# One transformer layer with a two-of-eight expert feed-forward: expert weight pieces placed singly in the last pass, raw rows kept in the next expert's slot, ranks and scatters moved forward

## The chip, the cores and the metric

The kernel runs on one core of one Trainium2 chip. Its time is the device time of one execution in microseconds (us); the number compared is the median over runs. The core has five engines with a queue each, which run their own instructions in order: TensorE (PE, with its weight loads shown as PEld), VectorE (DVE), ScalarE (ACT), GpSimd (POOL) and SyncE (SP, which here only issues transfers). They meet through semaphores alone.

## The reference, cut to what matters

There are 16 batches of 100 rows of width 512, and for each batch a context of 722 rows of width 384.

```python
x = x + self_attention(layernorm(x))            # 16 heads of 32, rotary, causal
x = x + cross_attention(layernorm(x), ctx_768)  # 16 heads of 32, keys and values from ctx
n = layernorm(x)
gates = softmax(n @ gate_w.T + gate_b)          # 8 experts
top_gates, top_idx = top_k(gates, 2)
expert_out = einsum('bsh,eoh->bseo', n, expert_w) + expert_b
x = x + (take(expert_out, top_idx) * top_gates).sum(experts)
```

## The kernel before, in words

**Passes.** The program is a software pipeline of passes n = -1 to 16. Pass n does the cross attention of batch n and prepares batch n+1 (self attention, keys and values of the context). Each pass is a list of 20 steps (`STEPS`, and for the last two `LAST_STEPS` and `END_STEPS`), and a step is a list of names. Every engine walks the same lists and runs its own part of each name, so the order in the lists is the order in each engine's queue, written out by hand. Pass 15 (`LAST_STEPS`) has no next batch to prepare. Pass 16 (`END_STEPS`) runs the feed-forward for the sorted rows.

**Cross attention of a pass.** It goes by four groups of four heads. For group g: `Ag` and `Bg` are the scores of the two halves of the context on PE (L1009); `max_Ag` and `max_Bg` are row maxima on DVE (L1268), which hold the score banks until they are read; `MXg` turns the joined maximum on PE (L911), ACT copies it (L1084) and DVE splits it (L1224); `Tga` and `Tgb` are the scores turned, each followed by `expga` or `expgb` on ACT (L1111). `highga`/`highgb` (ACT, L1120) and `lowga`/`lowgb` (POOL, L1442) split the probabilities into two half-precision parts, and `PVg` multiplies them with the values (PE, L921). `A` of the next group waits for both `exp` of this one. `PV3` of a pass, `scale_heads` (POOL, L1436), `TT` (turn the heads' output) and `TP` (its projection and the residual) stand in the next pass.

**Chunks.** The other PE work goes through four PSUM banks in turn (`filler`): PE writes a bank, ACT copies the high part, DVE forms the low part and counts `chunk_out`; a chunk's PE work waits until DVE is done with the chunk four before it.

**Experts' weights.** An expert's 512x512 float32 weights are loaded raw (`load_expert`), and four pieces `FWek` turn them on PE (four transposes each, L957), then ACT (L1093) and DVE (L1236) write their two half-precision parts into `wT_all`, the expert's slot in `bank`. Slot e takes the place of weights of the attention that are no longer wanted: slots 0 to 3 of the self attention's four matrices, 4 to 6 of the cross attention's, 6 and 7 of the keys of even passes. Experts 0, 1 and 2 lie raw in their own slot, so ACT waits for all four turned pieces before it writes the first; experts 3 to 7 lie raw in three other places that come free one after another. The pieces stand four at a time in `LAST_STEPS`.

**Routing.** Rows come in 13 tiles: 11 early ones (batches 0 to 13) and two late ones (batches 14 and 15). For tile t: `FSt` statistics (DVE), `FNt` normalising (POOL, L712 to L717), `FXt` turning (PE), `FLt` gate scores. When the eleventh tile is done, `RT00` to `RT03` and `RE0` take the softmax and the two best experts (DVE, L578 to L605; ACT), `RP` writes the picks, `FR` counts them on PE (L970, L973) and `dve_place` on DVE works out each row's place among 29 slot tiles sorted by expert (L627 to L646; L639 writes the places and counts `placed`). `SCt` on POOL (L690) then scatters tile t's normalised rows to DRAM, two indirect transfers a tile; SP brings the rows back into one of four buffers ahead of it (`load_again`), where tile t+4 waits until tile t is scattered. In pass 16 SP loads the sorted slots once all scatters have landed (`end_loads`, L468), and for each slot tile j `STj` (turn, L966) and `SMj` (product, L323) follow. After them come the two late tiles through all experts, and the sums.

## Time and profile before

| | us |
|---|---|
| median of 3 runs (lowest, highest) | 1288.94 (1286.7, 1290.46) |
| profiled execution, its own time | 1286.48 |
| its span, first to last instruction | 1284.7 |
| PE busy over the span | 1196.7 (93%) |
| DVE busy | 835.0 (65%) |
| POOL busy | 728.5 (57%) |
| ACT busy | 641.6 (50%) |

The profile is one execution. Busy shares are means over stages with different limits, so each stage has to be read by itself: passes -1 to 14 up to 1036 us, pass 15 from there to about 1120 us, pass 16 and the sums to the end. In the chain of waits each step stands at the instruction that ended last or at what released it, and "issue" is time in which an engine waited for nothing that the profile shows.

### The profile page before, as it was taken

To read this page: it belongs to the slowest core of one execution; us is meant where nothing else is said; L and a number is where in the kernel's file an instruction comes from. 1 tells how busy PE (TensorE), PEld (TensorE's weight loads), DVE (VectorE), ACT (ScalarE), POOL (GpSimd) and SP (SyncE) were. 2 spreads that over 40 slices of the span, in tenths; PEclk is the share of its full clock that TensorE was granted. 3 is DMA by queue.
4 is the path that set the end of the run, shared out by engine and by line. 5 is a ranking of instruction groups with operands and counts; after the bars stand their busy time and mean duration, and the time that the engine had idled before them with its cause. 6 is when DMAs were issued, how large, how long until landed. Compare 5 with 4: busy or idle time off the path is not lost.

```text
span 1284.7 us, 43326 instructions
## 1 busy us (share of the span) xinstructions
PE 1196.7 (93%) x19120; PEld 808.5 (63%) x19120; DVE 835.0 (65%) x1455; ACT 641.6 (50%) x946; POOL 728.5 (57%) x690
## 2 busy tenths in 40 slices
PE   4789999999999999999999999999999967599997
PEld 4456666666767676767676767576767655455543
DVE  4658486858686767677777776776777786323156
ACT  4335555556565656564746565555555545433300
POOL 1436666667676665758575757575757536510042
PEclk8799999999999999999999999999999978699999
DMA  8010611010101010110101010102020524545356
GB/s 301 1 42 2 239 44 50 2 59 9 60 17 52 17 44 11 50 37 32 49 20 51 18 53 7 58 3 66 3 66 22 176 72 150 194 152 170 128 166 212
DMA packets 47840, 93.28 MB, mean 73 GB/s; under 512 B 3775, under 2 KB 15351, under 8 KB 47655
## 3 DMA queue, kind: packets, MB, share of 16 engines
q1 hardware_dynamic: 44135, 79.03, 18.7%
q0 software_dynamic: 3520, 11.47, 2.8%
q8 instruction: 154, 2.52, 0.8%
q14 instruction: 31, 0.25, 0.1%
HBM read 60.13 MB, written 30.36 MB: 70 GB/s over the span
## 4 chain that ended last, share of the span: by engine, by line
PE 88%; DVE 4%; issue 2%; ACT 2%; POOL 1%; DMA 1%; SPq 0%; DVEq 0%; ACTq 0%
PE psum L323 57%; PE psum L921 7%; PE psum L1024 7%; PE psum L1009 5%; PE psum L939 2%; PE psum L898 2%; PE psum L890 1%; PE psum L957 1%; DMA bank<-in_L_attn_Wv 1%; PE psum L512 1%; PE psum L966 1%; PE psum L854 1%; PE psum L906 1%; DVE xT L1176 1%; DVE bank L1236 1%
## 5 line engine op out<-in xcount | busy, mean ns | idle before, releaser
L1442 POOL TENSOR_TENSOR bank<-prob,bank 128x1200 f16<-128x1200 f32 x128 | 314.5, 2468 | 184.7 <-ACT bank L1120 184.6
L1268 DVE TENSOR_REDUCE c_most<-psum 100x4 f32<-100x1444 f32 x128 | 211.5, 1653 | 15.8 <-PE psum L1009 13.7
L323 PE MATMUL psum<-bank,cT 128*128 128x512 f16 (+1 forms) x864 | 198.7, 379 | 0.0
L323 PE MATMUL psum<-cT,bank 128*128 128x361 f16 x1152 | 195.7, 321 | 0.0
L1111 ACT ACTIVATE prob<-psum 128x1200 f32<-128x1200 f32 x128 | 149.9, 1171 | 78.2 <-PE psum L1024 63.9
L1176 DVE TENSOR_TENSOR cv<-psum,cv 128x512 f16<-128x512 f32 x125 | 85.8, 688 | 112.0 <-ACT cv L1102 57.6
L1120 ACT ACTIVATE bank<-prob 128x1200 f16<-128x1200 f32 x128 | 151.7, 1198 | 1.4
L323 PEld LDWEIGHTS psum<-cT,bank 128*128 128x128 f16 x1152 | 106.0, 98 | 65.3 <-DVE c_raw L1195 3.3
L323 PEld LDWEIGHTS psum<-bank,cT 128*128 128x128 f16 (+1 forms) x864 | 85.1, 101 | 88.2 <-issue 3.8
L1102 ACT ACTIVATE cv<-psum 128x512 f16<-128x512 f32 x96 | 57.3, 597 | 153.3 <-PE psum L323 151.6
L1229 DVE SCALAR_TENSOR_TENSOR bank<-psum,b_part,bank 128x361 f16<-128x361 f32 x128 | 74.4, 592 | 80.8 <-ACT bank L1088 80.7
L1088 ACT ACTIVATE bank<-psum,b_part 128x361 f16<-128x361 f32 x128 | 72.0, 563 | 105.2 <-PE psum L323 105.2
L323 PE MATMUL psum<-xT,bank 128*128 128x100 f16 x2304 | 111.7, 208 | 10.2 <-DVE xT L1176 7.6
L323 PEld LDWEIGHTS psum<-xT,bank 128*128 128x128 f16 x2304 | 105.8, 98 | 16.8 <-DVE xT L1176 12.7
L921 PE MATMUL psum<-cv,bank 128*128 128x65 f16 (+1 forms) x3072 | 106.6, 194 | 4.6 <-issue 4.3
L921 PEld LDWEIGHTS psum<-cv,bank 128*128 128x128 f16 (+1 forms) x3072 | 101.5, 98 | 10.4 <-issue 6.7
L1009 PE MATMUL psum<-bank,cq 32*100 32x361 f16 x1536 | 87.0, 330 | 9.6 <-DVE c_most L1268 7.9
L1024 PE MATMUL psum<-cq,bank 32*128 32x100 f16 x4608 | 88.3, 207 | 6.6 <-issue 2.4
L323 PE MATMUL psum<-bank,xT 128*100 128x512 f16 x384 | 88.8, 381 | 0.0
L1024 PEld LDWEIGHTS psum<-cq,bank 32*128 32x128 f16 x4608 | 68.3, 94 | 31.0 <-issue 14.5
L323 PE MATMUL psum<-bank,cv 128*128 x348 | 80.8, 384 | 3.2 <-DVE cv L1176 3.2
L1429 POOL TENSOR_TENSOR c_raw<-c_raw,s_rinv 100x400 f32<-100x400 f32 x64 | 53.9, 853 | 41.3 <-DVE s_rinv L1337 41.3
(219 smaller groups left out, 1915.0 us busy)
## 6 DMA issues: line engine op xcount, KB each, us to landing
c_raw<-in_ctx SPq DMA_DIRECT2D x16, 960.0 KB
xs_scratch<-y_kept SPq DMA_DIRECT2D x1, 7424.0 KB, 22.9
c_raw<-xs_scratch SPq DMA_DIRECT2D x29, 256.0 KB, 2.7
ys_scratch<-bank SPq DMA_DIRECT2D x29, 256.0 KB, 2.0
x_in<-in_x SPq DMA_DIRECT2D x16, 200.0 KB
x_scratch<-x_out SPq DMA_DIRECT2D x16, 200.0 KB
bank<-in_L_ffn_expert_w SPq DMA_DIRECT2D x3, 1024.0 KB, 9.1
y_kept<-x_scratch SPq DMA_DIRECT2D x10, 256.0 KB, 3.2
```

Of the source, the lines that this page charges most:

```text
L323: last = pe.matmul(out_ap, a(pa), b(pb), start=(i == 0 and j == 0), stop=(i == len(pairs) - 1 and j == 2))
L921: last = pe.matmul(f[:, c * HV:(c + 1) * HV], prob16[i % 2][0:r, at:at + P], cv[odd][0:r, t, HT * i + c, 0:HV], start=t + p == 0, stop=t + ...
L1009: last = pe.matmul(score[0:L, c, 0:HC], cq[it.odd][rows, a, o], split_k[it.odd][rows, b, o, hf * HC:(hf + 1) * HC], start=i == 0, stop=i == 2)
L1024: last = pe.matmul(score[:, c, j * L:(j + 1) * L], minus[rows] if a is None else split_k[it.odd][rows, b, o, t * CW:(t + 1) * CW], max_spl ...
L1088: op = act.activation(split_k[not it.odd][:, 0, i // 2, (i % 2) * HC:(i % 2 + 1) * HC], f[:, 0:HC], ACT.Identity, bias=b_part[:, 3, i // 2 ...
L1102: op = act.activation(cv_half[not it.odd][0:r, i, :, 0], f[0:r, 0:D].rearrange("k (h d) -> k h d", h=H), ACT.Copy)
L1111: act.activation(prob[:, part].rearrange("k (c q) -> k c q", c=HT), score[:, :, 0:3 * L], ACT.Exp, scale=SOFT)\
L1120: act.activation(prob16[o % 2][:, part * PT:(part + 1) * PT], prob[:, part], ACT.Copy).then_inc(prob_high, 1)
L1176: return dve.tensor_tensor(dst, src, high, ALU.subtract)
L1229: op = dve.scalar_tensor_tensor(k[:, 1, i // 2, c], f[:, 0:HC], b_part[:, 3, i // 2:i // 2 + 1], k[:, 0, i // 2, c], ALU.add, ALU.subtract)
L1268: dve.tensor_reduce(c_most[:, hf], score[0:L, :, 0:HC], AXIS.X, ALU.max).then_inc(max_done, 1)
L1442: pool.tensor_tensor(prob16[o % 2][:, (2 + part) * PT:(3 + part) * PT], prob[:, part], prob16[o % 2][:, part * PT:(part + 1) * PT], ALU.su ...
```

## The change

The lists `GATE_EXTRA` and `LAST_STEPS` are written anew. In pass 14 `FS10` to `RP` come one or two steps sooner, and `FR` and `SC0` move from pass 15 into the last two steps of pass 14. In pass 15 the 32 pieces stand singly or in pairs in every step, `SC1` to `SC7` come sooner, and `PV3`, `scale_heads`, `TT` and `TP` come one to four steps later, `PV0` to `PV2` one step later. `dve_place` is cut in two: the part up to `placed` stays with `FR`, and the part that works out each slot tile's expert and the picked gates gets a name, `PL`, in step 3 of pass 15.

Each raw expert e now lies in slot e+1 (expert 7 in `c_flat`), so that turned pieces never overwrite their own raw rows, and ACT waits for its own piece alone. Experts 0 and 1 are loaded after `SV` of pass 14 as before, 7 after `SO`, 2 after `OP`, and 3 to 6 at the start of pass 15 when the last `exp` of pass 14 is done. `load_again` of tiles 4 to 7 follows these; the store of batch 14's rows and `load_y` of tile 11 stand around `load_again` of tile 8. The sorted slots wait for `FW73`, since they share `c_flat` with expert 7.

```diff
@@ -116,29 +116,29 @@
-GATE_EXTRA = {11: ["FS10"], 12: ["FN10"], 14: ["FX10"], 15: ["FL10"], 16: ["RT00", "RE0"], 17: ["RT01"], 18: ["RT02"],
-              19: ["RT03", "RP"]}
+GATE_EXTRA = {10: ["FS10"], 11: ["FN10"], 12: ["FX10"], 13: ["FL10"], 14: ["RT00", "RE0"], 15: ["RT01"], 16: ["RT02"],
+              17: ["RT03", "RP"], 18: ["FR"], 19: ["SC0"]}
 LAST_STEPS = [
-    ["low3a", "A0", "max_A0", "low3b", "FW00", "FW01", "FW02", "FW03"],
-    ["B0", "max_B0", "FW10", "FW11", "FW12", "FW13"],
-    ["MX0", "PV3", "FR"],
-    ["T0a", "exp0a", "scale_heads"],
-    ["T0b", "exp0b", "SC0", "high0a", "TT"],
-    ["A1", "max_A1", "low0a", "high0b", "FW20", "FW21", "FW22", "FW23"],
-    ["B1", "max_B1", "low0b", "TP"],
-    ["MX1", "SC1", "FW30", "FW31", "FW32", "FW33"],
-    ["T1a", "exp1a", "PV0", "SC2"],
-    ["T1b", "exp1b", "high1a", "FW40", "FW41", "FW42", "FW43"],
-    ["A2", "max_A2", "low1a", "high1b"],
-    ["B2", "max_B2", "low1b", "FS11", "SC3"],
-    ["MX2", "FW50", "FW51", "FW52", "FW53", "FN11"],
-    ["T2a", "exp2a", "PV1", "SC4"],
-    ["T2b", "exp2b", "high2a", "FX11"],
-    ["A3", "max_A3", "low2a", "high2b", "FL11", "FW60", "FW61", "FW62", "FW63"],
-    ["B3", "max_B3", "low2b", "SC5"],
-    ["MX3", "SC6", "FW70", "FW71", "FW72", "FW73"],
-    ["T3a", "exp3a", "PV2", "SC7"],
-    ["T3b", "exp3b", "high3a", "high3b", "SC8", "SC9", "SC10"],
+    ["low3a", "A0", "max_A0", "SC1", "FW00", "FW01"],
+    ["B0", "max_B0", "low3b", "FW02", "FW03"],
+    ["MX0", "SC2", "FW10"],
+    ["T0a", "exp0a", "PV3", "FW11", "PL"],
+    ["T0b", "exp0b", "high0a", "FW12", "FW13"],
+    ["A1", "max_A1", "low0a", "high0b", "FW20", "FW21"],
+    ["B1", "max_B1", "low0b", "scale_heads", "FW22", "FW23"],
+    ["MX1", "SC3", "FW30", "FW31"],
+    ["T1a", "exp1a", "SC4", "TT", "FW32"],
+    ["T1b", "exp1b", "high1a", "PV0", "FW33", "FW40"],
+    ["A2", "max_A2", "low1a", "high1b", "TP", "FW41"],
+    ["B2", "max_B2", "low1b", "FW42", "FW43"],
+    ["MX2", "SC5", "FW50", "FW51"],
+    ["T2a", "exp2a", "FS11", "SC6", "FW52", "FW53"],
+    ["T2b", "exp2b", "high2a", "PV1", "FN11", "FW60", "FW61"],
+    ["A3", "max_A3", "low2a", "high2b", "FW62", "FW63"],
+    ["B3", "max_B3", "low2b", "FX11", "FW70"],
+    ["MX3", "SC7", "FL11", "FW71"],
+    ["T3a", "exp3a", "SC8", "FW72", "FW73"],
+    ["T3b", "exp3b", "high3a", "PV2", "high3b", "SC9", "SC10"],
 ]
@@ -165,7 +165,7 @@
     [f"ST{j}" for j in range(SLOT_TILES)])
-FFN_KINDS = ("FS", "FN", "FX", "FL", "FG", "FW", "FR", "RT", "RE", "RP", "SC", "ST", "SM", "BV")
+FFN_KINDS = ("FS", "FN", "FX", "FL", "FG", "FW", "FR", "RT", "RE", "RP", "PL", "SC", "ST", "SM", "BV")
@@ -339,11 +339,8 @@
         y_again = [y_kept[:, (t + 3) % 4] for t in range(EARLY)]
-        raw_space = {"c": c_flat[:, 0:KD * D], "T": cT[:].rearrange("p k s c -> p (k s c)").bitcast(F32)[:, 0:KD * D],
-                     "v": cv_all[0].bitcast(F32)[:, 0:KD * D]}
-        raw_home = (None, None, None, "c", "T", "v", "T", "v")
-        raw_e = [(bank[:, e * KD * 2 * D:(e + 1) * KD * 2 * D].bitcast(F32) if raw_home[e] is None else
-                  raw_space[raw_home[e]]).rearrange("p (o h) -> p o h", o=KD) for e in range(E)]
+        raw_e = [(bank[:, (e + 1) * KD * 2 * D:(e + 2) * KD * 2 * D].bitcast(F32) if e < E - 1 else
+                  c_flat[:, 0:KD * D]).rearrange("p (o h) -> p o h", o=KD) for e in range(E)]
@@ -616,7 +613,7 @@
-            done = [0]
+            done = [0] if ranks is not None else [10]
@@ -624,6 +621,9 @@
             shape = [P, EARLY, E]
+            if ranks is None:
+                place_experts(dve, step)
+                return
             step(dve.tensor_tensor(over_steps[:], ranks[:, EARLY].unsqueeze(2).to_broadcast([P, E, EARLY]),
@@ -637,6 +637,10 @@
             dve.tensor_copy(slot_i[:], slot_f[:]).then_inc(placed, 1)
+            assert done[0] == 10
+        def place_experts(dve, step):
             step(dve.tensor_tensor(past[:], tile_no[:].unsqueeze(2).to_broadcast([1, SLOT_TILES, E]),
@@ -752,7 +756,7 @@
                 sp.wait_ge(chunk_out, it.done("SV"))
-                for e in range(3):
+                for e in range(2):
                     load_expert(sp, e)
@@ -766,37 +770,34 @@
                 load_y(sp, EARLY - 1)
-                sp.wait_ge(chunk_out, it.done("SO"))
-                load_expert(sp, 3)
                 store_y(sp, EARLY - 1)
...
                     load_again(sp, t)
+                sp.wait_ge(chunk_out, it.done("SO"))
+                load_expert(sp, E - 1)
+                sp.wait_ge(chunk_out, it.done("OP"))
+                load_expert(sp, 2)
...
             sp.wait_ge(chunk_out, it.all_before())
-            load_expert(sp, 4)
-            sp.wait_ge(chunk_out, it.done("PV3"))
-            load_expert(sp, 5)
-            sp.wait_ge(chunk_out, it.done("TP"))
-            sp.dma_start(x2_dram[B - 2], x_out[:]).then_inc(x2_stored, 16)
-            load_again(sp, 4)
-            load_y(sp, EARLY)
-            load_again(sp, 5)
-            sp.wait_ge(chunk_out, it.done("FW43"))
-            load_expert(sp, 6)
-            load_again(sp, 6)
-            sp.wait_ge(chunk_out, it.done("FW53"))
-            load_expert(sp, 7)
-            for t in range(7, EARLY):
+            sp.wait_ge(exp_done, 2 * GROUPS * (B - 1))
+            for e in range(3, E - 1):
+                load_expert(sp, e)
+            for t in range(4, EARLY):
+                if t == 8:
+                    sp.wait_ge(chunk_out, it.done("TP"))
+                    sp.dma_start(x2_dram[B - 2], x_out[:]).then_inc(x2_stored, 16)
                 load_again(sp, t)
+                if t == 8:
+                    load_y(sp, EARLY)
...
             all_scattered(sp)
-            sp.wait_ge(chunk_out, its[B - 1].done("FW33"))
+            sp.wait_ge(chunk_out, its[B - 1].done("FW73"))
             for j in range(4):
@@ -1066,8 +1067,7 @@
             kind, i = name[:2], int(name[2:]) if name[2:].isdigit() else 0
-            in_place = kind == "FW" and raw_home[int(name[2])] is None
-            act.wait_ge(chunk_ready, it.done(name[:3] + str(KD - 1) if in_place else name))
+            act.wait_ge(chunk_ready, it.done(name))
             if name in ("X1T", "X2T", "SO", "TT"):
@@ -1314,6 +1314,8 @@
                         dve_picks(dve)
+                    elif name == "PL":
+                        dve_place(dve, None)
                     elif name[:4] == "max_":
...
```

## Rows read from the trace of the kernel before

**Rows 1.** Windows: busy us of each engine (instructions), granted PE clock, DMA share, GB/s.
```profile
970.00:1036.00 66.00, 62.57 (x1145) 43.25 (x1137) 49.05 (x87) 35.53 (x53) 41.20 (x39) 1.00 0.29 96
1036.00:1059.00 23.00, 13.40 (x223) 10.71 (x219) 20.38 (x48) 7.20 (x13) 6.02 (x4) 0.72 0.27 93
1093.40:1125.60 32.20, 16.88 (x226) 13.53 (x226) 11.86 (x19) 13.23 (x19) 19.85 (x16) 0.67 0.53 176
1125.60:1218.00 92.40, 92.40 (x529) 50.59 (x530) 24.11 (x54) 30.64 (x57) 4.40 (x6) 0.99 0.47 154
```
**Rows 2.** Chain of waits, 1020 to 1130 us: start us, us, engine or issue, tile, line.
```profile
1029.60 0.71 PE psum L1024 x48
...
1037.43 2.40 DVE route_all L599
1043.41 1.57 DVE c_most L1268
...
1046.18 3.62 PE psum L957 x16
...
1069.01 1.92 PE psum L957 x16
...
1106.80 1.14 issue
...
1125.59 4.05 PE psum L323 x12
```
**Rows 3.** Waits, 1036 to 1126 us: us in total, times, longest.
```profile
PE psum L921 <- issue: 4.3, 7, 1.2
PE psum L1024 <- issue: 4.1, 5, 1.1
```
**Rows 4.** Groups by line, 1036 to 1126 us: busy us, mean ns, idle before.
```profile
L1442 POOL TENSOR_TENSOR bank<-prob,bank 128x1200 f16<-128x1200 f32 x10 | 24.5, 2462 | 19.5 <-ACT bank L1120 19.5
L690 POOL DMA_INDIRECT xs_scratch<-y_kept,slot_i x22 | 21.7, 989 | 8.3 <-issue 5.8 <-DVE slot_i L639 2.5
L1236 DVE SCALAR_TENSOR_TENSOR bank<-psum,bank 128x512 f16<-128x512 f32 x32 | 20.5, 685 | 9.5 <-ACT bank L1093 8.8 <-issue 0.6
...
L1268 DVE TENSOR_REDUCE c_most<-psum 100x4 f32<-100x1444 f32 x8 | 13.2, 1652 | 1.3 <-PE psum L1009 1.3
...
L1111 ACT ACTIVATE prob<-psum 128x1200 f32<-128x1200 f32 x8 | 9.4, 1172 | 20.5 <-remote 10.4 <-PE psum L1024 10.0
```
**Rows 5.** Timeline of PE: start us, us, operation, idle before.
```profile
1010.73 0.31 PE L1024 MATMUL psum<-cq,bank 32*128 32x100 f16 x12 [0.25 <-DVE max_split L1224]
...
1036.10 0.67 PE L1009 MATMUL psum<-bank,cq 32*100 32x361 f16 x12
```
**Rows 6.** Timeline of DVE.
```profile
1041.88 0.25 DVE L602 TENSOR_TENSOR route_all<-route_all,best 128x88 f32<-128x88 f32 x1
...
1057.20 0.18 DVE L639 CAST slot_i<-slot_f 128x22 int32<-128x22 f32 x1
```
**Rows 7.** Timeline of POOL.
```profile
1012.55 0.77 POOL L717 TENSOR_SCALAR y_kept<-y_kept,nmean,rstd 128x512 f32<-128x512 f32 x1
...
1054.18 1.05 POOL L1436 TENSOR_TENSOR c_out<-c_out,c_rinv 100x512 f32<-100x512 f32 x1 [14.47 <-DVE c_rinv L1262]
...
1084.86 0.25 POOL L712 TENSOR_SCALAR nmean<-moments 100x1 f32<-100x1 f32 x1 [0.70 <-DVE moments L1293]
...
1086.17 0.77 POOL L717 TENSOR_SCALAR x_norm<-x_in,nmean,rstd 100x512 f32<-100x512 f32 x1
...
1113.47 0.99 POOL L690 DMA_INDIRECT xs_scratch<-y_kept,slot_i  x1 [0.31 <-issue]
```
**Rows 8.** Timeline of SP's queue of transfers.
```profile
1116.81 9.20 SPq L468 DMA_DIRECT2D c_raw<-xs_scratch  x7
```
**Rows 9.** Transfers by line: count, KB each, median us from issue to landing.
```profile
c_raw<-xs_scratch SPq DMA_DIRECT2D x29, 256.0 KB, 2.7
...
bank<-in_L_ffn_expert_w SPq DMA_DIRECT2D x3, 1024.0 KB, 9.1
```

## The prediction, on record before the changed kernel ran

> **What bounds the kernel now.** I read the windows first. Up to 1036 us PE is busy 62.57 of 66 us at a granted clock of 1.00 (the upper of its two levels, 2.4 GHz), and from 1125.6 to 1218 all of 92.40 at 0.99 [rows 1]. Between them lies pass 15, some 90 us, in which no engine is full: 13.40 of 23.0 us for PE in its first group and 16.88 of 32.2 in its last, with the clock at 0.72 and 0.67, a mix of 1.2 and 2.4 GHz. So waits set pass 15, and PE's work sets what is around it. The chain of waits says which [rows 2]. PE starts A0 at 1036.10 [rows 5], but max_A0 starts on DVE only at 1043.41, behind the routing, whose L599 alone takes 2.40. Four pieces at a time (3.62 at the low clock, 1.92 at the high one) then stand in front of the next link. At the end, from 1106.80, come stretches of "issue": PE holds work that waits for nothing shown and does not run it, 4.3 + 4.1 us in the window [rows 3], while POOL issues its last scatters. The chain reaches pass 16's first product (SM0) at 1125.59. What must be over by then is the scattering: the last of 22 is issued at 1113.47 + 0.99 = 1114.46 [rows 7], and SP may load slots from 1116.81 [rows 8]. The scatters begin when `placed` is counted, at 1057.20 + 0.18 = 1057.38 [rows 6]. After SM0 PE never waits, so what SM0 gains the end gains.
>
> **Part 1, routing sooner in pass 14.** Let t0 be the start of T3a in pass 14, 1029.60 before [rows 2]. FX10 now stands on PE ahead of T2a, which began at 1010.73 [rows 5]; but its normalised rows are ready at 1012.55 + 0.77 = 1013.32 [rows 7], and POOL's queue up to there is unchanged. PE stands still and T2a starts after FX10 (0.6, estimated as four transposes, a little over a fourth of the 1.92 for sixteen), at about 1013.9: +3.2. FX10 is no longer paid later: -0.6. RT02 (six instructions) now stands on DVE ahead of the max_split that releases T3a, where it costs 6 x 0.25 = 1.5 alone [rows 6] or up to 2.40 for one when it meets a POOL split of 2.46 [rows 2, 4]; part of it lies in a wait that was there for RT00, so I take +0.4. t0 becomes 1029.6 + 3.0 = 1032.6. Bounds: 0 (POOL happens to be early) and +6.
>
> FR then waits on PE for RT03 and RP, some 14 DVE instructions at 0.25 after max_split, 3.7 us with the two others between; CQ hides all but about 1.6 of it. FR itself and the ten steps of placing take 0.7 and 3.3, and one of them meets POOL's split of the queries. So `placed` is at t0 + 8.1 = 1040.7, and A0 at t0 + 8.3 = 1040.9. Before, these were 1057.38 and 1036.10: A0 is 4.8 later, `placed` 16.7 sooner. DVE reaches max_A0 with almost no backlog (0.5 us).
>
> **Part 2, POOL from `placed` to the last scatter.** This is the sum that decides. Work: 22 scatters, each 0.99 and 5.8 / 21 = 0.28 of issue behind it, 28.0 [rows 4]; eight splits (3a and 3b of pass 14, 0 to 2 of pass 15) at 2.46, 19.7 [rows 4]; `scale_heads` 1.05; FN11, from 1084.86 to 1086.94, 2.1 [rows 7]. Together 50.9. Idle: at least 0, at most the 19.5 us for which the splits waited on ACT in pass 15 before [rows 4]. To choose, I walk the other chain. A bare group is two halves (0.67 + 1.65) [rows 4, 5], two turned scores with exp (0.71 + 1.17) [rows 2, 4] and about 1.5 for the turned maximum, 9.9 us. Eight pieces are 8 x 0.685 = 5.5 on DVE [rows 4]; each half has two of them in front of its maximum or its split, and PE's TP (2.8 by the kernel's other projections), PV and pieces stand over the short exp waits. I take 3.6 of fill, 13.5 a group. A3 then starts at 1040.9 + 3 x 13.5 = 1081.4; low2b, two splits and the copies behind exp2b, ends about 4.7 later at 1086; eight scatters follow it (SC7 to SC10), 10.2. That is 1096.3, or 4.7 of idle; rounding up for FN11, which waits for tile 11's rows to be stored and read back, I take 6.0. Last scatter issued: 1040.7 + 50.9 + 6.0 = 1097.6, against 1114.46: 16.9 sooner.
>
> **Part 3, the tail to SM0.** Before, 1125.59 - 1114.46 = 11.1 us: 2.35 until SP passes, then 8.8, in which the slots land (2.7 [rows 9]) but ACT still has exp3b and two copies to do. Now exp3b is done before the last scatter has landed, so 2.7 and three short links (0.6 each, estimate) are left, about 4.9, unless PE is starved again. Between 4.9 and 8.8 I take 7.4: a gain of 1.4.
>
> **Part 4, what costs nothing.** Raw rows in the next slot: three loads of 1 MB land within 9.1 us of issue in the median [rows 9]; experts 3 to 6 start at about 1042 and are wanted from step 7, some 20 us later. This cover is gone if scatters halve the rate: expert 6 would still be in by about 1075 and is wanted after 1075. `PL`, some 2 us on DVE, stands beside PV3. Loading two experts instead of three ahead of the store of batch 13 lets tile 10's rows come sooner, so FS10 does not wait. `FW73` ahead of the slots: done long before the last scatter.
>
> **Sum.** 16.9 + 1.4 = 18.3, rounded to 18: SM0 at 1107.6. The profiled execution took 1286.48 (span 1284.7 and 1.8 around it); it would take 1268.5. The median shown lies 2.46 above it, so 1288.94 - 18 = 1271.
>
> **A rule weighed against the trace.** "Issue" on PE totals 8.4 us in pass 15, nearly all from 1106.80 while scatters flow [rows 2, 3]. The Trainium skill, "Runtime: NRT & Kernel Launch", section "Instruction fetch mechanics", says an engine fetches instructions in blocks of 16 KiB while it executes and that crossing a block is mostly hidden. By that rule scatters cost PE nothing, the 8.4 us have another cause, and the sum would be 18. The same skill, "DMA: Bandwidth & Descriptors", section "Queues, rings and completion order", says each DMA engine takes turns between queues a packet at a time, by which fetches would stand behind scatters; by it the rivals 2 and 3 hold. The row sides with the second.
>
> **Rivals.** 1, a cold attention chain. If PE runs at 1.2 GHz through pass 15, a group grows: sixteen transposes cost 3.62 instead of 1.92 [rows 2], so 3.4 for a group's 32, and its scores 4 x 0.45; half of the sum is on the chain, 2.6 to 3.3. Three groups: 10 us. Time 1281. For it: 0.72 and 0.67 before. Against: the low clock followed standstills on PE that single pieces fill.
> 2, mild starvation. 14 scatters now lie ahead of low2b among dense PE work. At 8.4 / 12 = 0.7 us each (the last twelve stood in one row) that is 9.8 on the chain. Time 1281. Against: pairs before showed next to none.
> 3, slower than before. The same mechanism, with four loads of 1 MB in flight beside the first scatters, holding all engines. Place: groups 0 to 2. From 22 us, 1.6 for each of 14 scatters, the gain is used up; at 2 us each, 28, the time is 1299. Against: it is more than a scatter's own 1.27.
> 4, the change does not do what it says: raw rows, tile 10 or tile 11 come late and queues stand in order behind them. A wait of some 9 us for a set of loads [rows 9] in each of two places uses the gain up: 1289. Against: the dates of part 4.
> 5, better: POOL idles little and t0 moves by less than 1 us: 18 + 6 + 2 = 26, 1263 or below.
>
> **How the numbers follow.** Forecast 0.60 (gain 13 to 24: 1265 to 1276, its own range); rival 1 0.14; rival 2 0.08; rival 5 0.06; rival 4 0.05; rival 3 0.07. What can be told from no change is 0.3%, 3.9 us. Faster: 0.60 + 0.14 + 0.08 + 0.06 = 0.88; same 0.05; slower 0.07. The range runs from rival 5 to rivals 1 and 2, 1262 to 1282; t0's bounds and the idle's, 6 below to 13 above, lie in it but for the last 2 us.
>
> **What would show it.** Right: a PE wait ahead of FX10 of about 2 to 3 us in pass 14; `placed` near 1041; the last scatter near 1098; POOL busy for over 85% of the time between; SM0 near 1107; the clock nearer 1.00 in pass 15. Wrong: scatters done long before SM0 (then the attention chain is the bound); more than 10 us of PE "issue"; pieces waiting for loads; anything changed after SM0.

## The result, and the profile after

The changed kernel takes 1280.48 us (median of 5 runs, 1280.13 to 1282.69) against 1287.42 of the kernel before beside it (1285.81 to 1290.46): a ratio of 0.9938, 95% interval 0.9926 to 0.995. It is faster by about 7 us where 18 were forecast; the time lies inside the range of 1262 to 1282, near rival 2's 1281. The profiled span went from 1284.7 to 1278.7.

Windows of the changed kernel, columns as in [rows 1]: pass 14 from 970, the four groups of pass 15, and what follows SM0.
```profile
970.00:1036.00 66.00, 58.65 (x972) 38.96 (x968) 48.14 (x86) 31.22 (x49) 38.93 (x37) 0.97 0.29 96
1045.00:1060.80 15.80, 10.29 (x210) 8.24 (x207) 9.43 (x17) 6.60 (x11) 11.08 (x8) 0.89 0.83 307
1060.80:1079.70 18.90, 12.98 (x213) 10.46 (x213) 11.19 (x22) 11.28 (x17) 11.38 (x8) 0.82 0.45 163
1079.70:1094.60 14.90, 11.67 (x222) 8.71 (x221) 11.37 (x18) 9.21 (x15) 9.03 (x10) 1.00 0.46 149
1094.60:1120.70 26.10, 15.61 (x222) 11.61 (x221) 11.14 (x18) 12.09 (x18) 17.39 (x12) 0.67 0.39 123
1120.70:1213.00 92.30, 92.28 (x535) 50.84 (x536) 24.73 (x54) 31.06 (x59) 3.20 (x6) 1.00 0.48 156
```
Up to 1036 PE lost some 4 us of busy time against [rows 1]. The last group before SM0 is 26.1 us at a clock of 0.67, with as many PE instructions (222) as the group of 14.9 before it and nearly twice its work on POOL (17.39 against 9.03). After SM0 nothing changed: 92.3 us, full.

Waits of PE, 1008 to 1122 us, and below them of ACT, 1045 to 1122 us (us in total, times, longest), which answer to [rows 3] and [rows 4]:
```profile
PE psum L1025 <- DVE max_split L1224: 3.9, 2, 3.3
PE psum L1025 <- issue: 2.8, 5, 1.2
PE psum L963 <- POOL y_kept L721: 2.8, 1, 2.8
...
PE psum L958 <- issue: 1.6, 3, 0.8
```
```profile
ACT prob L1111 <- remote: 10.4, 2, 7.0
```
Below, a hold is the time by which an instruction starts or ends late though nothing that the profile shows keeps it, and a row is a number of scatters that POOL issues with no other work of POOL between them. The holds of before are still there: PE waits 5.2 us in this window for nothing that is shown (4.4 in these two lines), and ACT's exp waits 10.4 for "remote", in all as much as in [rows 4], where it was one wait. Where they stand, the timeline of PE and then of ACT shows (start us, us, operation, idle before):
```profile
1103.58 0.44 PE L1025 MATMUL psum<-cq,bank 32*128 32x100 f16 x12
...
1105.40 0.25 PE L1025 MATMUL psum<-cq,bank 32*128 32x100 f16 x1 [0.45 <-issue]
...
1106.14 0.24 PE L1025 MATMUL psum<-max_split,minus 32*128 32x100 f16 x1 [0.45 <-issue]
...
1112.55 0.44 PE L1025 MATMUL psum<-cq,bank 32*128 32x100 f16 x12 [3.16 <-ACT prob L1111]
```
```profile
1111.33 1.17 ACT L1111 ACTIVATE prob<-psum 128x1200 f32<-128x1200 f32 x1 [7.04 <-remote]
```
A T needs 0.7 us at the upper clock when nothing holds it and 1.18 at the lower (T3b, from 1112.55, at a granted clock of 0.50). Here T3a runs from 1103.58 to 1106.38, 2.8 us, and exp3a, for which no other wait is shown, starts 4.95 us after its end. POOL meanwhile issues the last row of eight scatters, and exp3a starts 1.57 us after the last one:
```profile
1099.69 1.12 POOL L694 DMA_INDIRECT xs_scratch<-y_kept,slot_i  x1 [0.16 <-issue]
...
1108.76 1.00 POOL L694 DMA_INDIRECT xs_scratch<-y_kept,slot_i  x1 [0.30 <-issue]
```
T1a (1.9 us, its exp 2.16 late) and T2a (2.1 us, its exp at once) are held in the same way beside the two rows of four scatters. The pairs in the first group, which have a split between them, hold next to nothing (T0a 0.78, T0b 0.72).

The chain of waits shows what SM0 waited for at the end of pass 15, and it is not the scatters: exp3a is followed on ACT and DVE by the copies of the last pieces, and SP passes its wait for `FW73` (L800) when they are done, 4.6 us after POOL's last issue ended at 1109.76.
```profile
1103.71 7.59 another core or an unknown queue
...
1111.33 0.14 ACT prob L1111
...
1113.02 1.30 DVE bank L1236 x2
...
1114.33 0.03 SPq L800
```
The other lines that answer to rows of before: POOL's groups [rows 4], then single instructions of POOL, PE, DVE and SP's queue [rows 5 to 8].
```profile
L1444 POOL TENSOR_TENSOR bank<-prob,bank 128x1200 f16<-128x1200 f32 x10 | 24.5, 2464 | 18.3 <-ACT bank L1120 18.2
L694 POOL DMA_INDIRECT xs_scratch<-y_kept,slot_i x22 | 21.8, 993 | 7.6 <-issue 5.7 <-DVE slot_i L639 2.0
```
```profile
1012.59 0.77 POOL L721 TENSOR_SCALAR y_kept<-y_kept,nmean,rstd 128x512 f32<-128x512 f32 x1
```
```profile
1013.50 0.63 PE L963 MATMUL psum<-ident,y_kept 128*128 128x128 f32 x4 [2.81 <-POOL y_kept L721]
1014.07 0.31 PE L1025 MATMUL psum<-cq,bank 32*128 32x100 f16 x12
...
1035.58 0.44 PE L1025 MATMUL psum<-cq,bank 32*128 32x100 f16 x12 [3.29 <-DVE max_split L1224]
...
1036.70 4.18 PE L323 MATMUL psum<-xT,bank 128*128 128x100 f16 x48
...
1045.08 0.67 PE L1010 MATMUL psum<-bank,cq 32*100 32x361 f16 x12
...
1120.72 1.47 PE L323 MATMUL psum<-bank,cv 128*128 x6 [0.47 <-issue]
```
```profile
1031.70 2.33 DVE L576 TENSOR_TENSOR route_all<-route_all,best 128x88 f32<-128x88 f32 x1
...
1044.57 0.18 DVE L639 CAST slot_i<-slot_f 128x22 int32<-128x22 f32 x1
```
```profile
1114.40 7.55 SPq L465 DMA_DIRECT2D c_raw<-xs_scratch  x7
```

### The profile page after: what moved, and what is told of

Read it like the earlier page. It is cut to its first block, busy times and chain, and to the rows that moved or that the text cites. A ratio compares the mean times of both kernels' runs of the same rounds, so it can differ in the third digit from the quotient of the medians.

```text
span 1278.7 us, 43327 instructions
## 1 busy us (share of the span) xinstructions
PE 1194.4 (93%) x19120; PEld 806.8 (63%) x19120; DVE 830.7 (65%) x1455; ACT 642.2 (50%) x946; POOL 729.6 (57%) x690
## 4 chain that ended last, share of the span: by engine, by line
PE 86%; DVE 4%; DMA 3%; POOL 3%; ACT 2%; issue 1%; another core or an unknown queue 1%; SPq 1%; ACTq 0%; DVEq 0%
PE psum L323 56%; PE psum L922 7%; PE psum L1025 6%; PE psum L1010 5%; PE psum L940 2%; PE psum L899 2%; PE psum L891 1%; DMA bank<-in_L_attn_Wv 1%; DMA out<-bank 1%; PE psum L967 1%; PE psum L855 1%; PE psum L907 1%; DVE xT L1176 1%; POOL bank L1444 1%
## 5 line engine op out<-in xcount | busy, mean ns | idle before, releaser
L1268 DVE TENSOR_REDUCE c_most<-psum 100x4 f32<-100x1444 f32 x128 | 211.6, 1653 | 14.7 <-PE psum L1010 12.6
L323 PEld LDWEIGHTS psum<-xT,bank 128*128 128x128 f16 x2304 | 108.4, 99 | 16.6 <-DVE xT L1176 12.7
```

The costliest lines, as they stand in the source:

```text
L323: last = pe.matmul(out_ap, a(pa), b(pb), start=(i == 0 and j == 0), stop=(i == len(pairs) - 1 and j == 2))
L1268: dve.tensor_reduce(c_most[:, hf], score[0:L, :, 0:HC], AXIS.X, ALU.max).then_inc(max_done, 1)
```

## The experiments

Times are medians; "before" is the kernel before, measured beside it on the same chip. A0, A3 and SM0 are starts in one profiled execution. A0 of pass 14, up to which all these kernels do the same, lies between 969.3 and 974.3 us in them, so such dates of two runs can differ by 5 us without the edit. Holds are read from each run's timeline: T takes 0.7 us (1.18 at the lower clock) and its exp starts 0.05 after it when undisturbed.

| kernel | us | before, us | ratio, 95% | A0 | A3 | SM0 |
|---|---|---|---|---|---|---|
| u_clumps | 1280.49 | 1287.86 | 0.9944, 0.9932 to 0.9957 | 1045.17 | 1097.50 | 1123.14 |
| u_routing | 1283.17 | 1287.86 | 0.9959, 0.9944 to 0.9975 | 1036.80 | 1089.84 | 1121.56 |
| few_rows | 1280.87 | 1287.86 | 0.9947, 0.9932 to 0.9961 | 1042.59 | 1095.80 | 1121.38 |
| lows_first | 1281.59 | 1287.86 | 0.9953, 0.9936 to 0.997 | 1044.79 | 1096.81 | 1122.31 |
| pool_dummy | 1270.04 | 1290.06 | 0.9846, 0.9831 to 0.9861 | 1044.98 | 1089.78 | 1110.03 |
| fx_later | 1278.37 | 1290.06 | 0.9903, 0.9887 to 0.9919 | 1043.93 | 1095.26 | 1121.45 |
| y11 | 1283.47 | 1290.06 | 0.9945, 0.993 to 0.9959 | 1044.58 | 1095.29 | 1122.46 |
| mix | 1281.78 | 1290.06 | 0.9938, 0.9922 to 0.9953 | 1038.56 | 1092.41 | 1120.17 |
| spread | 1278.05 | 1288.34 | 0.9918, 0.9904 to 0.9932 | 1046.16 | 1094.78 | 1117.52 |
| spread_fx | 1272.73 | 1288.34 | 0.9873, 0.9858 to 0.9888 | 1040.83 | 1089.49 | 1112.19 |
| pool_plain | 1270.05 | 1288.34 | 0.9854, 0.9839 to 0.9868 | 1047.40 | 1089.32 | 1110.44 |
| last_dummy | 1276.69 | 1288.34 | 0.991, 0.9896 to 0.9924 | 1041.96 | 1092.67 | 1112.51 |
| pairs | 1275.94 | 1289.64 | 0.9882, 0.9862 to 0.9902 | 1047.09 | 1098.31 | 1118.73 |
| pairs_fx | 1273.15 | 1289.64 | 0.9877, 0.986 to 0.9895 | 1039.12 | 1088.93 | 1109.38 |
| pairs_rt | 1275.47 | 1287.91 | 0.9905, 0.9891 to 0.9919 | 1039.00 | 1091.96 | 1113.16 |
| plain_fx | 1266.13 | 1287.91 | 0.9829, 0.9815 to 0.9844 | 1041.29 | 1081.90 | 1103.98 |

**Parts undone.** u_clumps puts the pieces back, four at a time; u_routing puts routing, places and scatters back, and moves the store and load around tile 11 ahead.
```diff
# u_clumps
-    ["low3a", "A0", "max_A0", "SC1", "FW00", "FW01"],
+    ["low3a", "A0", "max_A0", "SC1", "FW00", "FW01", "FW02", "FW03"],
...
# u_routing
-    ["MX0", "SC2", "FW10"],
-    ["T0a", "exp0a", "PV3", "FW11", "PL"],
+    ["MX0", "FW10", "FR", "PL"],
+    ["T0a", "exp0a", "PV3", "FW11"],
...
-    ["MX1", "SC3", "FW30", "FW31"],
+    ["MX1", "FW30", "FW31", "SC1"],
```


> The changed kernel with its pieces four at a time again (at the steps of the kernel before); routing, places, scatters and raw rows as changed. Theory A (the attention chain makes POOL wait, and four pieces in front of a link lengthen it): 2 to 3 us more for each of three groups, 1286 to 1290 us, A1 to A2 and A2 to A3 each longer than in the changed kernel. Rival B (the scatters that start sooner are the whole gain, POOL's own work is the bound): 1280 to 1282 us, as the changed kernel.

> The changed kernel with the routing, the places (FR, PL in step 2) and the scatters back at the steps of the kernel before; single pieces and raw rows as changed; the store and load around tile 11 one place sooner so that they don't wait for a late scatter. Theory A (pass 14 lost about 9 us to the routing's new places, which eats what the sooner scatters bring): A0 back at 1036 to 1037 us, placed at 1050 to 1054, the last scatter within 2 us of the changed kernel's 1109.8, 1279 to 1284 us. Rival B (the sooner scatters are the gain): 1286 to 1289 us.

Both intervals overlap that of the whole change, so neither half can be told from the two together: u_clumps came out as its rival B had it, and u_routing inside its theory's range. Neither takes the holds away: T3a takes 4.15 us in u_clumps; in u_routing exp3a is 11.14 late, beside its last row of scatters. That the halves don't add up fits an end which holds bound in both; these two runs alone don't show it.

**Bytes, then the scatters themselves.** few_rows scatters 16 rows of each tile instead of 128 (the others are left out). pool_dummy puts a POOL subtraction of about the same length in place of each scatter: nothing is scattered.
```diff
# few_rows, pool_scatter
-            n = tile_rows(t)[1]
+            n = 16
# pool_dummy, pool_scatter
-                pool.indirect_dma_start(xs_dram[:, :], bass.IndirectOffsetOnAxis(ap=slot_i[0:n, i, t:t + 1], axis=0),
-                                        y_again[t][0:n], None).then_inc(scattered[t % 4], 16)
+                pool.tensor_tensor(y_again[t][0:n], y_again[t][0:n], y_again[t][0:n], ALU.subtract).then_inc(scattered[t % 4], 16)
...
```


> The changed kernel with each scatter moving 16 rows of a tile instead of 128 (most sorted rows stay zero; everything else is computed), so that the scatters are issued as before but move an eighth. Theory A (while several scatters are in flight, PE and ACT run their queues in small doses): issue on PE in pass 15 under 1.5 us in place of 5.9, exp1a and exp3a start within 0.3 us of their scores in place of 2.2 and 4.9 us, SM0 6 to 10 us sooner, 1270 to 1275 us. Rival B (the scatters cost POOL's time alone): at most 1 us from landing sooner, 1279 to 1281 us, the late exps stay.

> The changed kernel with each of the 22 scatters replaced by a POOL subtraction on the same rows (about 1.1 to 1.3 us each, so POOL's queue is as full; nothing is scattered, the sorted rows stay zero). Theory C (it is POOL's issuing of indirect transfers that holds PE and ACT, whatever they move): T1a and T3a take 0.7 to 1.2 us instead of 1.9 and 2.8, exp1a and exp3a start within 0.3 us of them, issue on PE under 1 us, SM0 6 to 10 us sooner than in the changed kernel, 1270 to 1275 us. Rival D (the holds come from PE's and ACT's own instruction streams at that place): the holds stay, 1278 to 1281 us.

With an eighth of the rows T3a still took 7.24 us, T1a 3.43 and T2a 2.22. Without the indirect instructions none of them took over 1.2, every exp followed within 0.08, and the median fell by 10 us (ratio 0.9846 against 0.9938), with POOL as busy as in the change (44.7 us from `placed` to the last one, against 44.3). Waits of PE in few_rows, 1036 to 1122 us:
```profile
PE psum L1025 <- issue: 7.5, 15, 1.2
```
PE's timeline there shows the shape of a hold: from 1105.26 to 1111.77 a matmul or two at a time, mostly 0.70 us apart, while POOL issues one scatter every 1.15 and for 2.4 us after its last (the last line, POOL's):
```profile
1109.43 0.24 PE L1025 MATMUL psum<-cq,bank 32*128 32x100 f16 x1 [0.43 <-issue]
1110.13 0.26 PE L1025 MATMUL psum<-cq,bank 32*128 32x100 f16 x1 [0.47 <-issue]
1110.84 0.27 PE L1025 MATMUL psum<-cq,bank 32*128 32x100 f16 x2 [0.45 <-issue]
...
1108.53 0.85 POOL L694 DMA_INDIRECT xs_scratch<-y_kept,slot_i  x1 [0.30 <-issue]
```

**Indirect or plain.** pool_plain keeps the DMAs on POOL's own queue, at the same steps and with the same bytes, but writes each tile to a fixed place: rows stand at wrong slots.
```diff
-                pool.indirect_dma_start(xs_dram[:, :], bass.IndirectOffsetOnAxis(ap=slot_i[0:n, i, t:t + 1], axis=0),
-                                        y_again[t][0:n], None).then_inc(scattered[t % 4], 16)
+                pool.dma_start(xs_dram[(2 * t + i) * P:(2 * t + i) * P + n], y_again[t][0:n]).then_inc(scattered[t % 4], 16)
```


> Each indirect scatter becomes a plain DMA from POOL of the same tile to a fixed place, so rows stand at wrong slots: as many bytes, same queue, same steps. If it is the indirect form (its offsets) that holds PE and ACT: holds gone, SM0 near 1110, median 1268 to 1274, as with the subtractions. If any DMA that POOL issues in rows does it: holds stay, median 1277 to 1283.

No hold: 1270.05, no "issue" line among PE's waits and no "remote" among ACT's from 1036 to 1122 us. T3a (1097.16 to 1098.34, at the lower clock) and exp3a (at 1098.38) stand inside the row of eight plain DMAs (1095.15 to 1099.59) and are not held. A plain DMA takes POOL 0.57 us instead of 0.99, but that is not what brings the gain: pool_dummy, with POOL as busy as in the change, has the same time. Transfers between 1044 and 1112 us by queue (packets, MB, share of 16 engines), first of the changed kernel, then of pool_plain, then of few_rows (1042 to 1112):
```profile
q0 software_dynamic: 1760, 5.74, 23.0%
q8 instruction: 7, 0.11, 0.8%
```
```profile
q0 software_dynamic: 1760, 5.74, 23.6%
q8 instruction: 7, 0.11, 0.7%
```
```profile
q0 software_dynamic: 704, 0.72, 4.1%
q8 instruction: 6, 0.10, 0.6%
```
q0 carries what POOL issues. The same 1760 packets and 5.74 MB, and as many instruction packets, go with holds in the changed kernel and without in pool_plain; an eighth of the bytes goes with holds of 7 us. So it is the indirect instruction that holds the others, and neither its transfer nor the fetching of code. Of the two rules that the prediction set against each other, the first (the Trainium skill, "Runtime: NRT & Kernel Launch", section "Instruction fetch mechanics": crossing a block is mostly hidden) agrees with these rows, but what the prediction drew from it, that scatters then cost PE nothing, does not follow. The second, with which the prediction sided (the same skill, "DMA: Bandwidth & Descriptors", section "Queues, rings and completion order": engines take turns between queues) is not what holds PE here, since in pool_plain the same packets stand on the same queue and hold nothing.

**One row of them.** last_dummy replaces the last eight scatters alone (SC7 to SC10; their tiles are not scattered) by subtractions on a semaphore of their own, for which SP waits instead.
```diff
             for i in range(2):
+                if t >= 7:
+                    pool.tensor_tensor(y_again[t][0:n], y_again[t][0:n], y_again[t][0:n], ALU.subtract).then_inc(dummied, 1)
+                    pool.wait_ge(dummied, 2 * (t - 7) + i + 1)
+                    continue
```


> Only the last row of eight scatters (SC7 to SC10) becomes eight POOL subtractions; rows of those tiles are not scattered. If the row beside T3a holds T3a and exp3a by itself: their 7 us go, the holds of T1a, exp1a and T2a (2.1, 2.2, 1.4) stay, SM0 near 1114, median 1273 to 1276. If the holds come from elsewhere (a fetch at those places of the code, as a rival has it): T3a stays held and the median is 1279 to 1282.

T3a took 1.19, as long as it takes at the lower clock, and its exp came at once; T1a kept 1.71 with exp1a 2.16 late, T2a 2.07. So the row of eight held what stood beside it, and the holds beside the other rows stayed. The median is 0.7 us above the range expected.

**Order on POOL.** lows_first puts the splits low3a and low3b ahead of SC0 to SC2. spread deals the pairs out over ten steps; pairs puts each pair behind another POOL operation. The lines are those of pairs; spread has SC3, SC7 and SC10 behind high0a, high2a and high3a, which are ACT's, so that POOL met rows of four there.
```diff
-    ["low3a", "A0", "max_A0", "SC1", "FW00", "FW01"],
+    ["low3a", "SC1", "A0", "max_A0", "FW00", "FW01"],
...
-    ["MX0", "SC2", "FW10"],
+    ["MX0", "FW10"],
...
-    ["A1", "max_A1", "low0a", "high0b", "FW20", "FW21"],
+    ["A1", "max_A1", "low0a", "SC3", "high0b", "FW20", "FW21"],
...
-    ["T3b", "exp3b", "high3a", "PV2", "high3b", "SC9", "SC10"],
+    ["T3b", "exp3b", "high3a", "PV2", "high3b"],
```


> The changed kernel with POOL's low3a and low3b ahead of SC0 to SC2 (SC0 in step 1, SC1 and SC2 in step 2 of pass 15). Theory A (POOL's order makes PV3, and so T0b and the next groups, wait): PE's wait of 1.85 us ahead of PV3 goes, A1 is 2 to 4 us sooner, 1277 to 1279.5 us. Rival B (POOL's work is the bound and its order moves nothing): 1280 to 1281.5 us.

> Same work as the changed kernel; only the scatters are dealt out otherwise: one pair behind each of ten POOL splits of the last pass instead of rows of 4, 4 and 8. If rows of scatters back to back are what holds PE and ACT (pairs that had a split between them, in the changed kernel's first group, held nothing): the holds before and after T1a, T2a and T3a (2.1+2.2, 1.4, 2.1+4.9 us above the undisturbed 0.7 and 0.05) go, the last scatter ends near 1101, SM0 starts near 1112 and the median is 1270 to 1275. If any scatter near a score holds it, however spaced: each of T1a to T3a still waits 1 to 2 us and the median is 1278 to 1282.

> Same work as the changed kernel, scatters again dealt out otherwise. In spread POOL still met rows of four (SC2 with SC3, SC6 with SC7, SC9 with SC10), since the high halves are no POOL work and part nothing; T0b, T2a and exp3a beside them were held by 2.1, 1.8 and 3.9 us. Here one pair stands behind each low split, scale_heads and FN11, and the last behind low2b. By the theory that an indirect row over two is what holds: no hold over 0.5 us is left on T and exp of the last pass, the last scatter ends near 1099, SM0 near 1110, median 1270 to 1273. If pairs hold too, only less: T1a to T3a keep 1 us each, median 1274 to 1277. If the earlier scatters merely move the hold to A or B: those are late, median as spread (1278).

lows_first made a row of six at the start: T0a was held 1.2 us and the time was that of the change. spread missed its 1270 to 1275; its 0.9918 is below the change's 0.9938, but the intervals overlap, so a gain is not shown. What is still held there stands beside the rows of four, T0b 2.81, T2a 2.50, exp3a 3.93 late, and beside two pairs with `scale_heads` between them, T1b 1.91. pairs is clearly faster (0.9882, at most 0.9902). It missed its 1270 to 1273 too and fell into the range for pairs that hold less. It left T1a at 1.39, T2a at 1.90 and exp1a 0.72 late: shorter rows hold less, but pairs are not free. Its profiled run had the clock at 0.72 to 0.80 in all four groups, and its SM0 (1118.73) is that of the slowest of its four times.

**The start of pass 15.** fx_later moves FX10 and FL10 of pass 14 a step later, out of the wait for FN10; y11 moves tile 11's chunks later; mix does both and puts the ranks (RT02 to FR) a step later. spread_fx, pairs_fx and plain_fx are fx_later's edit on spread, pairs and pool_plain; pairs_rt has mix's ranks on pairs.
```diff
-GATE_EXTRA = {10: ["FS10"], 11: ["FN10"], 12: ["FX10"], 13: ["FL10"], 14: ["RT00", "RE0"], 15: ["RT01"], 16: ["RT02"],
-              17: ["RT03", "RP"], 18: ["FR"], 19: ["SC0"]}
+GATE_EXTRA = {10: ["FS10"], 11: ["FN10"], 13: ["FX10"], 14: ["FL10", "RT00", "RE0"], 15: ["RT01"], 16: ["RT02"],
+              17: ["RT03", "RP"], 18: ["FR"], 19: ["SC0"]}
# mix and pairs_rt: 17: RT02, 18: RT03 RP, 19: FR SC0
```


> The changed kernel with FX10 and FL10 one step later in pass 14 (steps 13 and 14), all else as changed. Theory E (PE's stand-still of 2.81 us ahead of FX10 pushes all that follows): it is gone, T2a at 1010.8, t0 and A0 2 to 3 us sooner, 1277.5 to 1279 us. Rival: RT02 and the split of POOL ahead of T3a take the time back, 1280 to 1281 us.

> The changed kernel with tile 11 later in pass 15 (FS11 in step 15, FN11 after low2b, FX11 in step 18, FL11 in step 19). Theory (POOL's wait of 2.53 us for tile 11's rows stands on the chain to the last scatter): low2a ends 2 to 4 us sooner, the last scatter at 1106 to 1108, 1277 to 1279 us. Rival (low2a waits for high2a anyway): no change, 1280 to 1281.

> As y11, and in pass 14 FX10 in step 13, FL10 with RT00 in 14, RT01 in 15, RT02 behind T3a's maximum in 17, RT03 and RP in 18, FR in 19. If the routing's place in pass 14 is what moved A0 9 us, t0 is back at 1030 to 1031, A0 at 1037 to 1039, placed at 1041 to 1042 and the last scatter 5 to 7 us sooner, 1273 to 1276 us. If DVE's backlog only moves to max_A0: 1278 to 1281 us.

> The pairs dealt out as in spread, and FX10, FL10 a step later in pass 14 (13 and 14 instead of 12 and 13), so that PE doesn't wait for FN10. By the theory of rows: 1268 to 1273, up to 3 us below spread. If t0 is given back by the later ranks: the same as spread. If spacing does nothing: 1277 to 1281.

> pairs with FX10 and FL10 at steps 13 and 14 of pass 14 instead of 12 and 13. Beside spread_fx (1272.7) the last scatter comes some 4 us sooner and the holds go: 1266 to 1270. If FX10's step was worth what spread_fx showed by chance: the same as pairs within 2 us.

> pairs_fx with RT02 at step 17 of pass 14 instead of 16, RT03 and RP at 18, FR and SC0 at 19. In the profiles of the changed kernel and of spread_fx a DVE subtraction of RT02 that takes 0.25 us elsewhere took 2.33 and 2.40 us beside a POOL split, and T3a of pass 14 waited 3.3 us for DVE's max_split behind it. If that wait is on the path: T3a 1.5 to 2 us sooner, FR and placed no later than in pairs_fx, median 1 to 2 us below it (1270 to 1273). If the ranks, one step later, become the last: FR waits for RP, A0 as in pairs_fx or later, median as pairs_fx or up to 3 us above.

> pool_plain (each scatter a plain DMA from POOL to a fixed place, rows at wrong slots) with FX10 and FL10 of pass 14 a step later. Both terms that the forecast missed are taken away together. If they are separate and the whole of the miss: pool_plain's 1270 less the 4 us that the later FX10 gave before A0, so 1265 to 1268. If they overlap (the later ranks given back where scatters no longer hold): 1269 to 1271.

From A0 of pass 14 to A0 of pass 15 the kernel before takes 66.6 us, the changed one 75.3; fx_later, spread_fx, pairs_fx and plain_fx take 69.7, 70.2, 69.8 and 70.6. Nine other kernels with the change's lists for pass 14 take 71.9 to 75.6, so the edit is worth some 1 to 6 us there. fx_later alone gives 0.9903, outside the change's interval (its profiled run was its slowest and began pass 14 4.4 us later than the change's, so its SM0 is no sooner). Against the kernel without the edit, measured beside it, the edit is worth 5.3 us (spread to spread_fx, intervals apart) and 2.8 (pairs to pairs_fx, intervals that overlap). pairs_fx missed its 1266 to 1270, and the holds did not go: T1a 1.74, T1b 2.17, exp3a 2.36 late. y11 and mix brought nothing, though A0 came sooner in mix: exp3a was held 6.4 us in both. In pairs_rt the wait for max_split went (0.2 us is left of 3.3), as expected, but B0 waited 3.2 us for DVE's maximum, which stands behind the later ranks (0.85 in pairs_fx), and the median is 1275.47: the rival of that run, that the later ranks give it back. PE also stood 2.15 us in "issue" ahead of 1032.62 there, ten us before the first scatter, so not every "issue" comes from scatters. plain_fx fell inside its 1265 to 1268, as if the two missed terms were separate and added up; its interval and pool_plain's overlap a little. Windows of its pass 14 end, four groups and wait for SM0:
```profile
1008.00:1041.30 33.30, 29.74 (x525) 20.62 (x524) 24.24 (x61) 16.32 (x24) 15.05 (x15) 0.90 0.32 104
1041.30:1053.10 11.80, 8.59 (x203) 6.70 (x201) 9.33 (x18) 6.44 (x11) 8.44 (x8) 1.00 0.86 283
1053.10:1067.20 14.10, 10.63 (x213) 8.66 (x213) 11.27 (x22) 11.05 (x17) 8.07 (x8) 0.88 0.87 324
1067.20:1081.90 14.70, 11.68 (x220) 8.61 (x219) 10.79 (x17) 9.81 (x15) 7.82 (x9) 1.00 0.49 154
1081.90:1104.00 22.10, 14.71 (x223) 11.71 (x222) 11.49 (x20) 11.70 (x17) 15.01 (x14) 0.73 0.43 143
```
The best that computes everything are spread_fx (1272.73) and pairs_fx (1273.15), both some 16 us below the kernel before and, by the ratios, 8 below the change.

## Why the prediction was wrong

Its own dates, as forecast, in the changed kernel, and in two kernels without indirect scatters (their last subtraction or plain DMA in the fourth line; A0 of pass 14 starts at 969.83 in the changed kernel, 972.10 in pool_dummy, 970.68 in plain_fx):

| | forecast | after | pool_dummy | plain_fx |
|---|---|---|---|---|
| t0 | 1032.6 | 1035.58 | 1037.42 | 1031.97 |
| placed | 1040.7 | 1044.75 | 1045.05 | 1041.14 |
| A3 | 1081.4 | 1094.59 | 1089.78 | 1081.90 |
| last issue ends | 1097.6 | 1109.76 | 1103.7 | 1092.1 |
| SM0 | 1107.6 | 1120.72 | 1110.03 | 1103.98 |
| time | 1271 | 1280.48 | 1270.04 | 1266.13 |

SM0 missed by 13.1 us: 4.05 up to `placed` (part 1), 8.1 from there to the last scatter (part 2), 0.96 in the tail (part 3).

**Part 2 is the step that failed.** Its work is as forecast: 22 scatters at 0.993 and 5.7 / 22 behind each (27.5 against 28.0), eight splits at 2.464 (19.7), 1.04 and 2.1, together 50.3 against 50.9. The idle, taken as 6.0, is 65.0 - 50.3 = 14.7: POOL waits 11.8 for ACT's halves, whose exp came late, and 2.5 for tile 11's statistics. Groups took 15.7, 18.9 and 14.9 where 13.5 was walked. pool_dummy has the same POOL work without the indirect form, and 58.7 us from `placed` to its last subtraction against 65.0: by these two profiles 6.3 of the 8.1 are the holds that POOL's own scatters put on PE and ACT, the rest the chain. The step went wrong in costing a scatter as POOL's time alone. Rival 2 had the mechanism. Its 0.08 rested on "pairs before showed next to none", which was a misreading: in the kernel before T2a stands beside one pair, takes 1.80 us and has its exp 0.76 late (POOL's timeline, then PE's):
```profile
1087.11 1.12 POOL L690 DMA_INDIRECT xs_scratch<-y_kept,slot_i  x1 [0.16 <-issue]
1088.54 0.95 POOL L690 DMA_INDIRECT xs_scratch<-y_kept,slot_i  x1 [0.31 <-issue]
...
1089.12 0.23 PE L1024 MATMUL psum<-max_split,minus 32*128 32x100 f16 x2 [0.49 <-issue]
```
And the change lays its pairs in rows of four and eight, because the high halves written between them are no POOL work. That its 1281 was met is partly chance: of the holds on T and exp 4.7 us (T1a, exp1a, T2a) lie beside the 14 scatters that it counted, where it had 9.8, some 6.5 (T3a, exp3a) beside the last eight, and 4 of the missing us are part 1's.

**Part 3** gave 0.1 where 1.4 was taken (10.96 from the last scatter to SM0, 11.1 before). It took the landing of the last scatter as what SP waits for, and the chain shows another path: exp3a, held to 1111.33, kept back the copies of the last pieces, and SP passed at 1114.33, when `FW73` was done. With the 2.35 us from the last issue to SP's start of before, SP could have started near 1112.1, an estimate, so `FW73` cost some 2.2 us. Behind it the slots needed 6.3 us to SM0 where 7.4 was taken (its lower bound was added wrongly: 2.7 and three times 0.6 make 4.5, not 4.9). In pool_dummy, where nothing has to land, the tail is 6.3 in all.

**Part 1.** The wait ahead of FX10 came as worked out (2.81, T2a at 1014.07 against 1013.9). t0 is 3.0 later than forecast, and A0 4.2. RT02 had been given 0.4; its subtraction took 2.33 beside a POOL split (1031.47 to 1033.92), so T3a waited 3.3 where it had waited 1.6 before, and CQ's 48 matmuls behind it took 4.18 at a clock of 0.50, the lower level, against 2.30 before. Both stand in spread_fx too (3.28 and 3.90), where FX10 doesn't wait, so they are not FX10's. FX10's own wait also costs clock: from 1010 to 1020 PE is busy 7.19 of 10 us at 0.83 (9.96 at 1.00 in spread_fx). From A0 of pass 14 to t0 the kernel before takes 60.1 us, the change 65.8 (64.2 to 67.2 in the nine kernels with its lists), pairs_fx, without FX10's wait, 61.4, and pairs_rt, without RT02's either, 58.2. So the two standstills of 2.8 and 3.3 us are worth some 3 to 6 and 3 there; FX10's had been costed at its own length.

**Part 4** held for the rows: no piece waits for them in the waits above, and nothing moved after SM0. Its last sentence, `FW73` "done long before the last scatter", failed: it was done 4.6 us after the last issue and was what SP waited for (part 3).

**The signs.** PE's wait, 2.81, and an unchanged end came as named. "More than 10 us of PE issue" did not come (5.2), and yet the holds were there: more than half of them show on ACT, as "remote". That sign looked at one engine where the cost falls on two. POOL was busy 77% of its stretch with the gaps behind scatters counted in, as in the sum (68% without them), not 85.

**Rival 1** is partly true: in pool_dummy the first two groups took 15.8 and 15.4 at a clock of 0.78 with no hold in them. But plain_fx had 0.73 in its last group and still reached SM0 16.7 us sooner than the change, so the cold clock is not the main loss. That pool_dummy lands on 1270 beside the forecast 1271 is partly chance: its A0 is 4.1 late, of which 2.6 lie ahead of pass 14 (972.10 against 969.53 before), and its tail 3.7 short.

**Open.** Why an indirect instruction on POOL holds other engines' queues, how long a row may be before it does, and what ends a hold; why T is held more than A and B. The kernel before has such holds too [rows 3, 4], 5.5 us on T3a and exp3a 5.6 late, so the change moved them and did not add them; how fast it would be without them was not measured.

## What to carry to other kernels

When scatters or gathers with offsets are moved, cost them on every engine that runs beside them, not on POOL alone: look for short dependent operations that wait for "issue" or "remote" while POOL issues a row, and test it with a plain DMA in place of the indirect one. Deal such instructions out in pairs with real work of the same engine between them (pairs still held some; single ones were not tried); a chunk of another engine in the written order parts nothing. Ask of every wait at the end of a stage, as SP's for `FW73`, what a late link ahead of it would do. And a standstill put on an engine that was full can cost more than its own length, as FX10's did, when the granted clock falls after it.

## What was not expected of the hardware

A row of indirect DMAs on POOL lets PE through in doses (in few_rows a matmul or two, mostly 0.70 us apart), whether a DMA moves 128 rows or 16, and ACT's exp beside it comes late: exp3a 1.57 us after the row's last issue in the changed kernel, but 1.4 before its end in y11 (1111.74 against 1113.11), so the end of the row is not what sets it free. Plain DMAs of the same bytes on the same queue do neither, and take POOL 0.57 us each instead of 0.99. In this kernel that form costs 11 to 12 us of 1280 (ratio 0.9846 or 0.9854 without it, 0.9938 with it).
